# Moving a two-batch kernel's setup into its first attention stage

## What is computed

```python
x = x + _layernorm(_L0_attn_ref(_layernorm(x), wq, wk, wv, wo))   # 16 heads, causal + local window
x = x + _layernorm(_L0_ffn_ref(_layernorm(x), W_fc, W_proj))      # ternary weights, relu^2, rms norm
x = x + _layernorm(_L1_attn_ref(_layernorm(x), W_in, W_out, ...)) # state-space mixer, 64 heads
x = x + _layernorm(_L1_ffn_ref(_layernorm(x), factors, bias))     # sum of 8 factors
```

```python
wb = w.astype(jnp.bfloat16)
scale = jnp.clip(jnp.mean(jnp.abs(wg), axis=-1, keepdims=True), 1e-08, None)
q = jnp.clip(jnp.round(wg / scale), -1.0, 1.0)
```

## Time and profile before

| | us |
|---|---|
| Median of three runs | 1797.98 (1793.96 to 1803.11) |
| The profiled execution, its own time | 1803.51 |
| Its span, first to last instruction | 1801.7 |
| PE busy | 1399.0 (78%) |
| DVE busy | 1166.2 (65%) |
| ACT busy | 924.9 (51%) |
| POOL busy | 277.8 (15%) |

### The profile page before, as it was taken

How to read it: one execution, slowest core, us unless ns; L and a number is a source line. 1 busy time by engine, 2 the same in 40 slices (tenths; PEclk the granted TensorE clock), 3 DMA queues, 4 the chain that set the end, 5 groups by cost and what they waited for, 6 DMA issues and landing times.

```text
span 1801.7 us, 41575 instructions
## 1 busy us (share of the span) xinstructions
PE 1399.0 (78%) x15736; PEld 811.3 (45%) x15816; DVE 1166.2 (65%) x2039; ACT 924.9 (51%) x1557; POOL 277.8 (15%) x268
## 2 busy tenths in 40 slices
PE   0368898595789999998526789886866999999982
PEld 0253332142446666666425333322433666666652
DVE  7457773324558889987555577514255889888936
ACT  0282455432557777775307345552334777777640
POOL 7320000011112222221012000001102222222200
PEclk9678999888779999999858699987966999899996
DMA  5300000100142222220010000001005222222100
GB/s 168 101 1 3 2 2 2 47 0 13 45 86 58 50 53 52 47 54 18 1 49 1 2 2 2 2 1 47 12 1 118 49 48 58 47 47 58 37 1 24
DMA packets 36850, 63.29 MB, mean 35 GB/s; under 512 B 15073, under 2 KB 24033, under 8 KB 35953
## 3 DMA queue, kind: packets, MB, share of 16 engines
q1 hardware_dynamic: 36432, 59.48, 13.4%
q10 hardware_dynamic: 288, 2.10, 0.3%
HBM read 20.79 MB, written 7.01 MB: 15 GB/s over the span
## 4 chain that ended last, share of the span: by engine, by line
issue 68%; PE 15%; POOL 5%; POOLq 4%; DVE 4%; ACT 3%; DVEq 1%; DMA 0%; ACTq 0%; SPq 0%
POOL region L661 3%; PE PS L1588 2%; POOLq L643 2%; PE PS L1604 2%; PE PS L1573 2%; PE PS L1548 1%; POOL region L635 1%; PE PS L1621 1%; PE PS L1546 1%; PE PS L1644 1%; ACT L859 1%; PE PS L1692 1%; PE PS L1545 1%; PE PS L1627 1%; PE PS L1560 1%
## 5 line engine op out<-in xcount | busy, mean ns | idle before, releaser
L661 POOL TENSOR_TENSOR region<-region 128x1024 f32<-128x1024 f32 x64 | 152.6, 2384 | 531.7 <-DVE region L1198 531.7
L1069 DVE TENSOR_REDUCE region<-PS 128x1 f32<-128x512 f32 (+3 forms) x304 | 180.4, 652 | 80.3 <-PE PS L1374 44.0
L742 ACT ACTIVATE region<-PS 128x512 f32<-128x512 f32 x288 | 164.1, 597 | 128.5 <-PE PS L1421 87.2
L1310 PE MATMUL PS<-ident,S 128*128 128x128 f32 x128 | 35.0, 429 | 167.8 <-DVE S L966 164.8
L1588 PEld LDWEIGHTS PS<-region 64*64 64x64 f32 x4096 | 136.9, 135 | 40.7 <-issue 40.7
L1588 PE MATMUL PS<-region 64*64 64x64 f32 x4096 | 154.5, 224 | 0.0
L1371 PE MATMUL PS<-region 96*128 96x512 bf16 (+3 forms) x384 | 115.0, 350 | 24.1 <-DVE region L1069 15.9
L1421 PE MATMUL PS<-region 99*128 99x512 bf16 x288 | 113.4, 417 | 18.5 <-ACT region L742 17.5
L1195 DVE SCALAR_TENSOR_TENSOR region<-region,rows 128x1024 f32<-128x1024 f32 x64 | 82.2, 1284 | 66.6 <-PE PS L1627 48.2
L642 POOL TENSOR_TENSOR region<-region 128x512 f32<-128x512 f32 x28 | 35.4, 1265 | 553.5 <-ACT region L784 552.7
L851 ACT COPY region<-PS 128x512 f32<-128x512 f32 x128 | 74.7, 583 | 81.3 <-PE PS L1573 80.8
(11 more groups left out here) (258 smaller groups left out, 3000.0 us busy)
## 6 DMA issues: line engine op xcount, KB each, us to landing
region<-region SPq DMA_DIRECT2D x256, 128.0 KB, 2.3
region<-parts_scratch SPq DMA_DIRECT2D x8, 448.0 KB, 8.0
region<-in_L_ffn_factors_dram SPq DMA_DIRECT2D x2, 1024.0 KB, 7.1
X<-in_L_attn_x_dram SPq DMA_DIRECT2D x2, 1024.0 KB, 5.8
region<-w1T_scratch SPq DMA_DIRECT2D x2, 1024.0 KB, 4.9
region<-w2T_scratch SPq DMA_DIRECT2D x2, 1024.0 KB, 7.0
out_dram<-X SPq DMA_DIRECT2D x2, 1024.0 KB, 4.9
parts_scratch<-region SPq DMA_DIRECT2D x2, 768.0 KB, 3.2
```

Source lines behind the costliest of these rows:

```text
L661: nc.gpsimd.tensor_tensor(PB1[:, r], PB1[:, r], PB2, ALU.add).then_inc(s_bb, 1)
L742: nc.scalar.activation(PB[:, u % (2 * G0), :], PS[:, 2 + u % 2, :], ACT.Exp).then_inc(s_p, 1)
L1069: nc.vector.reduce_max(MB[:, h:h + nh, k0 // 4], src, AX).then_inc(s_smu, 1)
```

## The change

1. **Loads.** SP sends x of batch 0 first, then the seven inputs of the attention on a semaphore of their own (s_first), then 13 others, then the feed-forward weights. PE, ACT and DVE start on s_first. The factors are loaded after the attention of batch 0.
2. **POOL.** The constant tiles and the expansion of parameters (`loop_constants`) and the ternary weights (`ternary_weights`, up to now DVE's) are done by POOL during the attention of batch 0, behind its copies of k; the zeroing of UI, US and DEC comes behind them.
3. **Late constants.** The transposes of parameters and ternary weights, and their copies, lie on PE and ACT between the attention and the feed-forward block of batch 0. ACT copies straight into w1T and w2T, and SP reads the scratch back only for batch 1.
4. **DVE.** The scaling of w_out_s goes into the last `out1` of batch 0, the sum of the factors behind the second `norm_input` of batch 0.
5. **Loops over the batch** are Python loops, so the program is written out twice with b a constant. The inner loops stay.
6. **Batch 1.** Its x is loaded into a second tile XF once the first gated tile of batch 0 is done; `norm_input` reads XF, and POOL moves XF into X after it has filled KT and V.

```diff
@@ sync
+            sp.dma_start(X[:], xv(0)).then_inc(s_x, 16)
             for dst, src in (
-                (ident[:], ident_d), (cosq[:], cos_d), (sinq[:], sin_d), (masks_f, masks_d),
+                (ident[:], ident_d),
                 (wqkv[:, :, 0:256], wq.rearrange("(k p) n -> p k n", p=P)),
...
+                (cosq[:], cos_d), (sinq[:], sin_d), (masks_f, masks_d),
+            ):
+                sp.dma_start(dst, src, allow_slow_non_contiguous=True).then_inc(s_first, 16)
...
-            with sp.Fori(0, NB) as b:
-
-                sp.wait_ge(s_out, b * 16)
-                sp.dma_start(X[:], x[bass.ds(b, 1), :, :].rearrange("o (t p) c -> p (o t) c", p=P)).then_inc(s_x, 16)
+            for b in range(NB):
...
+                if b == 0:
+                    loop_constants()
                 sp.wait_ge(s_s, b * BLOCKS * NT + NT)
+                if b == 0:
+                    sp.dma_start(fac[:, 0], factors[:, 0:P, :].rearrange("r p e -> p r e")).then_inc(s_fac, 16)
+                    sp.dma_start(fac[:, 1], factors[:, P:, :].rearrange("r p e -> p r e")).then_inc(s_fac, 16)
...
+                if b + 1 < NB:
+                    sp.wait_ge(s_gg, b * NT + 1)
+                    sp.dma_start(XF, xv(b + 1)).then_inc(s_x, 16)
                 sp.wait_ge(s_res, b + 1)
@@ gpsimd
+            def loop_constants():
+                pool.wait_ge(s_qxt, NT)
+                pool.wait_ge(s_w, 16 * NLOAD)
...
+            def ternary_weights():
+                pool.wait_ge(s_wt, 32)
+                grp = lambda t: t.rearrange("p (g n) -> p g n", n=GROUP)
+                quarters = [(w, 1024 * q, 16 * q) for w in range(2) for q in range(2)]
+                for w, c, g in quarters:
+                    nc.gpsimd.tensor_copy(TWB[:, w, c:c + 1024], TW[:, w, c:c + 1024])
+                pool.drain()
+                for w, c, g in quarters:
+                    nc.gpsimd.tensor_scalar(TA[:, w, c:c + 1024], TWB[:, w, c:c + 1024], 0.0, None, ALU.max)
+                    nc.gpsimd.tensor_scalar(TR, TWB[:, w, c:c + 1024], 0.0, None, ALU.min)
+                    pool.drain()
+                    nc.gpsimd.tensor_tensor(TA[:, w, c:c + 1024], TA[:, w, c:c + 1024], TR, ALU.subtract)
+                    pool.drain()
+                n = GROUP // 2
+                while n:
+                    for w in range(2):
+                        a = grp(TA[:, w])
+                        nc.gpsimd.tensor_tensor(a[:, :, 0:n], a[:, :, 0:n], a[:, :, n:2 * n], ALU.add)
+                    pool.drain()
+                    n //= 2
...
+                for w, c, g in quarters:
+                    s = slice(c, c + 1024)
+                    nc.gpsimd.tensor_tensor(grp(TA[:, w, s]), grp(TWB[:, w, s]), wide(TH[:, w, g:g + 16]), ALU.subtract)
+                    nc.gpsimd.tensor_tensor(grp(TR), grp(TWB[:, w, s]), wide(TH[:, w, g:g + 16]), ALU.add)
+                    pool.drain()
+                    nc.gpsimd.tensor_scalar(TA[:, w, s], TA[:, w, s], 0.0, None, ALU.is_gt)
+                    nc.gpsimd.tensor_scalar(TR, TR, 0.0, None, ALU.is_lt)
+                    pool.drain()
+                    nc.gpsimd.tensor_tensor(TA[:, w, s], TR, TA[:, w, s], ALU.subtract)
+                    pool.drain()
+                    nc.gpsimd.tensor_tensor(grp(TA[:, w, s]), grp(TA[:, w, s]), wide(TG[:, w, g:g + 16]), ALU.mult)
+                    pool.drain()
+                    nc.gpsimd.tensor_tensor(TA[:, w, s], TA[:, w, s], TW[:, w, s], ALU.add)
+                    pool.drain()
+                    nc.gpsimd.tensor_tensor(TW[:, w, s], TW[:, w, s], TA[:, w, s], ALU.subtract)
+                    pool.drain()
+                pool.drain().then_inc(s_wq, 1)
...
                 pool.drain().then_inc(s_one, 1)
+                if b > 0:
+                    pool.wait_ge(s_x, (b + 1) * 16)
+                    nc.gpsimd.tensor_tensor(X[:], XF, onesc[:].unsqueeze(2).to_broadcast([P, NT, C]), ALU.mult)
+                    pool.drain().then_inc(s_xf, 1)
...
+                if b == 0:
+                    loop_constants()
+                    ternary_weights()
@@ scalar
+            def late_constants():
+                act.wait_ge(s_wtp, 1)
+                nc.scalar.copy(rows[:], PS[:, 4, 0:4 * PAIRS].rearrange("p (k r) -> p k r", k=4)).then_inc(s_rp, 1)
...
+                nc.scalar.copy(steps[0:112], steps_f)
+                nc.scalar.copy(heads, heads_f.rearrange("p (k c) -> p k c", k=4)).then_inc(s_kc, 1)
...
+                for u in range(8):
+                    act.wait_ge(s_wtp, u + 1)
+                    nc.scalar.copy(dst[u // 4][:, (u % 4) * 512:(u % 4 + 1) * 512], PS[:, u % 4, :]).then_inc(s_wtc, 1)
@@ vector
+                norm_input(XF if b else X)
+                dve.wait_ge(s_first, 16 * NFIRST)
...
+                        if b == 0 and i == NT - 1:
+                            dve.wait_ge(s_w, 16 * NLOAD)
+                            for k in range(DI // P):
+                                nc.vector.tensor_scalar(w_out_s[:, k, :], w_out_s[:, k, :], nw_s[:, k:k + 1], None, ALU.mult)
...
+                dve.wait_ge(s_xf, b)
                 norm_output(0)
                 norm_input()
+                if b == 0:
+                    dve.wait_ge(s_fac, 32)
+                    nc.vector.tensor_reduce(fsum[:], fac.rearrange("p k r e -> p k e r"), AX, ALU.add).then_inc(s_fs, 1)
@@ tensor
+            def late_constants():
+                pe.wait_ge(s_smu, npieces)
+                pe.wait_ge(s_p, nunits)
+                pe.wait_ge(s_og, NT)
+                pe.wait_ge(s_ex, 1)
...
```

More of the change, by code:

```diff
@@ L575, in _ @@
-            nc.gpsimd.memset(ones_r, 1.0)
-            pool.drain().then_inc(s_fzz, 1)
-            nc.gpsimd.memset(rate[0:64], 1.0)
-            nc.gpsimd.memset(onesc[:], 1.0).then_inc(s_zero, 1)
-            pool.wait_ge(s_w, 16 * NLOAD)
-            for w in range(2):
-                v = bb[:, w].rearrange("r h (i two) -> r h i two", two=2)
-                for half in range(2):
-                    nc.gpsimd.tensor_copy(ex[:, 2 * w, :, half, :], v[:, :, :, 0])
-                nc.gpsimd.tensor_scalar(ex[:, 2 * w + 1, :, 0, :], v[:, :, :, 1], -1.0, None, ALU.mult)
-                nc.gpsimd.tensor_copy(ex[:, 2 * w + 1, :, 1, :], v[:, :, :, 1])
@@ L675, in transposed_input @@
                                    PS[:, 6 + i % 2, 0:KC * P].rearrange("p (k t) -> p k t", k=KC)).then_inc(s_xt, 1)
[L677 to L678 removed]
+            act.wait_ge(s_first, 16 * NFIRST)
             nc.scalar.copy(identb[:], ident[:])
[L680 to L684 removed]
```

298 lines of the change are left out of this document (145 added, 153 removed).

## The result

| | before | changed | ratio |
|---|---|---|---|
| Median of the runs (first comparison) | 1800.55 (1793.96 to 1807.96, 4 runs) | 1747.78 (1739.91 to 1750.97, 4 runs) | 0.9703 [0.9663, 0.9743] |
| Span of the profiled execution | 1801.7 | 1738.1 | |

The account below looks back on a forecast made before the run. PE was taken as nearest to the bound in the attention, behind a serial setup. The terms -64.8 (start), -2 (between batches) and +26 (holds) sum to -41 us: 1757 us against the median of 1798, range 1724 to 1784.

Parts of the forecast that it names:

- The start: Setup before batch 0: with x as first DMA, DVE's statistics begin at about 7.1 instead of 71.91 us; -64.8 us.
- The holds in the attention: Attention of batch 0: DVE's operations wait out POOL's instructions, so splits delay PE; +26 us, low end 8, high end 50.
- The 4 us for L1115 and the local steps: Attention of batch 0: these DVE operations are held half a POOL instruction each and PE waits for part; 4 us.
- How much of a hold reaches the end: Attention splits: PE's later start absorbs 2.7 us of the 9.1 us added to a split, so PE stands for 6.4.
- The sign that the prediction named: Attention: splits of 8 to 11 us beside POOL, PE idle 5 to 7 us before L1410 two or three times.
- a term for the clock, 2 us: Attention: a PE that stood is in part granted 1.2 GHz behind it; 2 us.
- Between the batches: Batch 0 to 1: early x saves at most 10.8 us, but POOL's fills and copy hold DVE; -2 (0 to -10.8).
- Edits at nothing: Late constants, factor sum, w_out_s scaling, SP's extra issues and unrolling are hidden or free; unrolling 0 (-5 to +5).
- the first rival: Holds hardly reach PE: small operations slip between POOL's or PE catches up; attention cost 5 us, total 1730; chance 0.20.
- Rivals 2: Attention holds cost 40 to 60 us, through slower tensor_scalars, the clock and local steps; total 1780; chance 0.12.
- 3 (held reductions): Slower kernel: DVE's maximum reductions are held by POOL too; total 1831 if DVE advances only in turns; chance 0.05.
- Rival 4: Setup: the seven other inputs crowd x, so no early start; 10 us late gives 1767; no chance of its own.

Follow-up runs that it names:

- Experiments 7 and 8: Changed kernel with the ternary weights back on DVE ahead of batch 0: 1771.71 us, 0.9854; changed kernel with x behind all other setup loads: 1766.86 us, 0.9774.
- Experiment 9: Changed kernel, POOL's ternary arithmetic replaced by 80 additions of 1024 elements with a drain only behind every fourth: 1761.6 us, 0.9774.
- Experiment 3: Changed kernel, POOL's ternary arithmetic replaced by 68 tensor_scalars of 128x1024, each with a drain: 1733.2 us, 0.9621.
- POOL idle: Changed kernel with the whole ternary arithmetic on POOL left out: 1734.98 us, 0.9622.
- experiment 2: Changed kernel, POOL's ternary arithmetic replaced by 80 additions of 128x1024, each with a drain: 1757.09 us, 0.9755.
- experiment 5: Changed kernel without POOL's copy of XF into X; norm_output of batch 1's first block adds to XF: 1741.29 us, 0.9648.
- experiment 6: Changed kernel with x of batch 1 loaded late into X, behind batch 0's store, without XF and POOL's copy: 1751.57 us, 0.9716.
- Experiment 10: Changed kernel without the XF copy, POOL's fills waiting for the last residual step, x of batch 0 in two DMAs: 1732.99 us, 0.9619.
- experiment 4: Kernel before the change with only its five batch loops written out: 1803.44 us, 1.0016.
- the two later medians: Changed kernel run again without an edit, in the second and third group: 1741.27 us, 0.9675, and 1733.49 us, 0.9646.

## Why the prediction came out as it did

**The start: right.** -65.35 against -64.8, and PE's transposes at 13.74 against 14.5. Experiments 7 and 8 show that both halves of it count: the setup's arithmetic gone (37.6 us for the ternary weights alone), and x first in the queue (18.5).

**The holds in the attention: mechanism right, size wrong.** This is the term that failed: "With POOL busy without a gap each of the five waits out one instruction", 10.3 us a split, +26 us. Splits beside POOL took 1.3 to 6.2 us, and the window grew by 6.6 (5 to 9 over three executions of the changed kernel, from 275.8). That is under the prediction's own low end of 8. Of it only the waits can be put down to the holds: PE was idle 58 us instead of 54 to 56, 2 to 4 us more. The rest is within the scatter of its busy time. Two parts of that sentence were wrong.
- POOL is not without a gap. Nearly every step of `ternary_weights` ends in a drain, and the pause of 0.14 us lets every second DVE operation through, because the one behind a held operation is issued some 0.1 us after POOL's end, just before POOL starts again. Experiment 9 took most pauses away and got the predicted 8 to 9 us a split.
- POOL's tensor_scalar does not hold like an addition. It holds a DVE operation only until 1.07 us after its start, and a cast or tensor_scalar of DVE also in its last 1.0. Experiment 3 measured the whole of it: +3.1 us of window over an idle POOL, against +23.4 for the additions, and no more PE idle time than with POOL idle.

The 4 us for L1115 and the local steps were too dear as well. L1115 (L1173 in the changed kernel) was held for 2.0 us in all eight tiles together. The transpose of the local step, from SBUF to SBUF, is not held at all, as DVE's and POOL's timelines of experiment 2 show:

```profile
202.56 0.71 DVE L1095 STREAM_TRANSPOSE region<-region 128x512 f32<-128x512 f32 x1
```

```profile
201.24 2.35 POOL L641 TENSOR_TENSOR region<-region 128x1024 f32<-128x1024 f32 x1
```

Against that, one price was too low: the tensor_scalar takes 2.77 us, my upper bound, not 1.2. It made POOL's ternary part 125 us instead of 105, about one more split beside it. But those long instructions are the harmless ones. The Trainium skill (GPSIMD Engine Reference, Engine selection) has one-input work at roughly line rate on GpSimd. For tensor_scalar the rows here disagree: it is slower than two-input work of the same size, 2.77 against 1.90 to 2.36 us. A cast of that size took 1.03 us.

**How much of a hold reaches the end: right where it was met.** The prediction let 6.4 of 9.1 us through, all but 2.7 of each long split. Experiment 9 has such splits, and PE stood 4.6 us behind one of 8.5 us, as that rule gives. The sign that the prediction named, PE idle 5 to 7 us before `rows` two or three times, did not come in the changed kernel: its longest split, 6.2 us, left 0.85 us where the rule gives 2.3. Over the whole window, from POOL idle to few drains, 42.5 us more of held splits went with 32.3 us more of window, but only 20.4 of these are PE's idle time; 11.9 are matmuls that ran longer. The prediction had a term for the clock, 2 us; if these 11.9 are that term, which is not shown, it was too small for splits as long as it assumed. In the changed kernel itself no loss to the clock stands out from the scatter.

**Between the batches: too dear.** -7.6 instead of -2. The memset was to hold a step of the root for 3.5 us and did not: the root's tensor_scalars were over when it began, and the two-input steps run inside it unhindered. It did hold the first XN, a tensor_scalar, to its end. The copy took 3.7 us instead of 4.5 and did hold one XN, but on the path that was worth 1.8 (experiment 5). So the sum of 8.8 taken off was 3.2 in truth (10.8 - 7.6), or 3.6 against the written-out loop (10.05 us of wait for x in experiment 6, 6.4 of them won). Experiment 10 got 3.0 of it back.

**Edits at nothing: right.** Late constants, sum of the factors, unrolling (experiment 4). The scaling of w_out_s took 1.13 us at 267.70, with DVE waiting 15.77 us for PE behind it. The middle of batch 0 grew by 3.1 us. All of it lies in the loop over pairs of heads, 367.9 to 371.6 us, which the change touches only by the unrolling; the kernel before written out has 371.3 there, and the executions scatter up to 382.0.

**The rivals.** By its mechanism the first rival came true: small operations slip between POOL's. It gave +5 for the attention and -8 between the batches; measured were +6.6 and -7.6. The forecast of the total was helped by luck: its largest loss was four times too dear, and the first group's median, which it is measured against, is the highest of the three. Against the profiled execution's own time the forecast was 1762.5 and 1739.91 was measured: 22.6 us off, 19.4 of it the holds and 5.6 the stretch between the batches. Against the first median it looks better, 9 us; the two later medians, 1741.27 and 1733.49, lie on the side of the trace. The prediction held it possible at 0.20 and should have weighed it higher: the pauses of 0.14 us stood in the earlier trace rows (487.15 to 487.29), and there the two engines were read as taking turns with long DVE operations, each longer than a pause, while the operations of a split last 0.17 us. Rivals 2 (40 to 60 us of holds) and 3 (held reductions) are out; experiments 2 and 9 show that rival 2 was only some 8 to 17 us away with other instructions on POOL. Rival 4 is out: the seven inputs did not delay x.

## What to carry to other kernels

Setup that only later stages need is worth moving behind the first load even if the engine that takes it contends with a busy one: here 65 us came off the front for an attention 5 to 9 us longer, of which 2 to 4 are waits for held operations. Price such a hold for the shortest dependent chain on the other engine, by the kind of the intruding instruction and by the pauses between its instructions, not by its busy time. Read the cost as idle time of the engine that bounds the stage; a window's length also has that engine's speed in it, which here moved it by up to 8 us from run to run. A copy or fill that is "free" on an idle engine is not free at the moment when the other one prepares the next stage; start it before the stage's elementwise part.

## What the runs showed of the hardware

- POOL's tensor_scalar on 128x1024 takes 2.77 us in float32 and in bfloat16 alike; its tensor_tensor 1.90 to 2.36.
- A POOL tensor_tensor or copy holds short two-input, cast and tensor_scalar operations of DVE until it ends: operations on 128x16 end 0.03 to 0.04 us behind it. Beside a POOL tensor_scalar of 2.77 us held operations end 1.06 to 1.07 us after its start. Later on two-input operations run free, even when issued 0.03 us before its end (experiment 3). A cast or tensor_scalar runs free with 1.08 us to go (experiment 6) and is held to the end with 1.00 us or less (experiment 10).
- A POOL memset on 3 partitions (3.51 us) holds DVE's tensor_scalars to its end (L1061, and L1059 in experiment 10), but not its two-input operations of 0.17 us.
- DVE's reductions from PSUM (mean 652 ns) and its SBUF-to-SBUF transpose of 128x512 float32 (0.70 us) take the same time inside a POOL tensor_tensor as without one.
- In the attention POOL's own instructions were not lengthened by DVE's short ones: L680 takes 2.35 us beside the reductions and beside the split, as L661 did before.
